# Eight scatters, the first two shared tiles, two low parts and nine loads moved around the end of an attention stage

## The reference

```python
x = x + tanh(g_xattn[0]) * L0_xattn(layernorm(x), ctx, mask)
x = x + tanh(g_ffn[0])   * L0_ffn(layernorm(x))
x = x + tanh(g_xattn[1]) * L1_xattn(layernorm(x), ctx)
x = x + tanh(g_ffn[1])   * L1_ffn(layernorm(x))
# L0_ffn, 1600 tokens, 8 experts, F = 192
scores = sigmoid(x @ W_gate_router)
sel = top_k(scores + expert_bias, 2)          # two experts for each token
w = scores[sel] / (scores[sel].sum() + EPS)
out = silu(x @ Wg_s) * (x @ Wu_s) @ Wd_s      # shared expert, every token
out += w[j] * (silu(x @ Wg[e]) * (x @ Wu[e]) @ Wd[e])   # for both chosen e
```

## Time and profile before

| what | us |
|---|---|
| median of 3 runs | 849.26 (846.79 to 850.47) |
| the profiled execution's own time | 849.73 |
| its span in the trace | 847.9 |
| PE busy | 767.5 (91%) |
| DVE busy | 578.1 (68%) |
| ACT busy | 470.4 (55%) |
| POOL busy | 214.4 (25%) |

### The profile page before, as it was taken

The page is one execution under the profiler, slowest core; times in us unless marked ns, Lnnn a source line. Parts: engine busy times, 40 slices in busy tenths (PEclk is TensorE's granted clock), DMA queues, the critical chain, the costliest instruction groups (busy, mean ns, idle before and its releaser), DMA issues.

```text
span 847.9 us, 22220 instructions
## 1 busy us (share of the span) xinstructions
PE 767.5 (91%) x7992; PEld 600.1 (71%) x7992; DVE 578.1 (68%) x1774; ACT 470.4 (55%) x1015; POOL 214.4 (25%) x212
## 2 busy tenths in 40 slices
PE   5879999999999888599998669999999898889997
PEld 2547777777767665379996457677777676669996
DVE  3877777777777676475544778787888687575433
ACT  2455666566555466345662346666666575565553
POOL 2553322133232314700005444322411210100000
PEclk9999999999999999999999869999999999999999
DMA  7899878778776903723325787887987987300001
GB/s 194 175 228 215 165 166 166 153 161 177 158 180 129 219 19 111 204 72 110 119 89 133 136 160 166 190 177 150 200 175 169 202 167 160 81 2 2 20 20 39
DMA packets 153765, 117.87 MB, mean 139 GB/s; under 512 B 81574, under 2 KB 145170, under 8 KB 153650
## 3 DMA queue, kind: packets, MB, share of 16 engines
q1 hardware_dynamic: 146410, 107.93, 58.2%
q0 software_dynamic: 4096, 6.57, 3.2%
q10 hardware_dynamic: 3152, 1.96, 1.0%
HBM read 76.17 MB, written 38.30 MB: 135 GB/s over the span
## 4 chain that ended last, share of the span: by engine, by line
PE 68%; DVE 10%; DMA 6%; issue 5%; ACT 5%; SPq 4%; ACTq 1%; another core or an unknown queue 1%; POOL 1%; DVEq 0%
PE ps L1986 21%; PE ps L2130 8%; PE ps L2104 7%; PE ps L2153 6%; PE ps L2163 6%; DMA scr_q<-qp 3%; PE ps L2149 3%; PE ps L2187 3%; DVE mx L1590 2%; DVE ps L1586 2%; ACT prob L1020 2%; SPq L478 2%; DMA QS<-scr_q 2%; PE ps L2057 2%; PE ps L2428 1%
## 5 line engine op out<-in xcount | busy, mean ns | idle before, releaser
L1020 ACT ACTIVATE prob<-ps 128x400 f32<-128x400 f32 (+1 forms) x384 | 182.4, 500 | 94.1 <-PE ps L2153 84.1
L2130 PE MATMUL ps<-KS,QS 96*100 96x361 bf16 x512 | 165.1, 338 | 17.8 <-DMA QS<-scr_q 5.5
L1586 DVE CUSTOM_DVE_ANT_0 ps<-ps,biasq 100x361 f32<-100x361 f32 x256 | 135.2, 542 | 51.7 <-PE ps L2130 43.4
L1590 DVE TENSOR_REDUCE mx<-ps 100x1 f32<-100x361 f32 x256 | 127.1, 527 | 47.0 <-PE ps L2130 40.4
L2153 PEld LDWEIGHTS ps<-QS,KS 98*128 98x128 bf16 x1536 | 108.6, 100 | 52.0 <-issue 9.7
L2153 PE MATMUL ps<-QS,KS 98*128 98x100 bf16 x1536 | 133.3, 210 | 9.0 <-ACT prob L1020 5.3
L2104 PE MATMUL ps<-cT,wk 128*128 128x361 f32 x256 | 96.6, 487 | 8.2 <-PEq L2399 6.8
L2130 PEld LDWEIGHTS ps<-KS,QS 96*100 96x100 bf16 x512 | 63.7, 126 | 53.2 <-DVE mx L1590 14.5
L730 POOL TENSOR_TENSOR kp<-kr,kp 128x722 bf16<-128x722 f32 x32 | 48.7, 1523 | 185.2 <-ACT kp L991 184.9
L2163 PE MATMUL ps<-prob,V 128*17 128x100 f32 (+1 forms) x3072 | 81.9, 256 | 0.1
L2163 PEld LDWEIGHTS ps<-prob,V 128*17 128x17 f32 (+1 forms) x3072 | 66.6, 100 | 12.7 <-issue 8.9
(11 more groups left out here) (225 smaller groups left out, 1598.1 us busy)
## 6 DMA issues: line engine op xcount, KB each, us to landing
scr_k<-kp SPq DMA_DIRECT2D x93, 180.5 KB
KS<-scr_k SPq DMA_DIRECT2D x62, 270.8 KB, 3.8
cT<-in_ctxT SPq DMA_DIRECT2D x32, 361.0 KB
KS<-scr_k SPq DMA_DIRECT2D x62, 180.5 KB, 4.2
QS<-scr_q SPq DMA_DIRECT2D x60, 150.0 KB, 4.6
KS<-scr_k SPq DMA_DIRECT2D x62, 90.2 KB, 4.4
scr_q<-qp SPq DMA_DIRECT2D x42, 100.0 KB, 5.2
xg<-scr_x SPq DMA_DIRECT2D x32, 128.0 KB
```

What stands on the lines that cost most here:

```text
L1020: nc.scalar.activation(prob[0:KROWS[t], t, hg, :], ps[0:KROWS[t], c % 2, 0:HQ * S], ACT.Exp).then_inc(a["exp"], 1)
L1586: nc.vector.tensor_tensor_reduce(ps[0:S, banks[h % len(banks)], 0:S2], ps[0:S, banks[h % len(banks)], 0:S2], biasq[p][:, :], 1.0, -3.0e38, ...
L1590: nc.vector.reduce_max(mx[:, h:h + 1], ps[0:S, banks[h % len(banks)], 0:S2], axis=AX.X).then_inc(a["max"], 1)
L2130: mm(ps[0:S, banks[h % len(banks)], 0:S2], QS[p][0:SROWS, h, :], KS[p][0:SROWS, h * S2:(h + 1) * S2], start=True, stop=True).then_inc(a["s ...
```

## The change

- **Scatters.** Steps 14 and 15 of the first attention issue four scatters each instead of two (0 to 15 are then done inside attention). POOL's wait for the end of attention goes away; scatters 16 to 25 come next, then the normalization constants of pair 7, then 26 to 31.
- **First tiles.** PE does `up(0)` and `up(1)` around the last batch's `turn_o`, ahead of `turn_on` and `project_o`; ACT loads the Silu table after `high_piece(4)` (by a Silu on one column) and does `silu(0)` before `copy_on`; DVE does `gate_up(0)` between pieces 3 and 4, ahead of the last `add_attention`.
- **Low parts.** All 12 are on DVE: 3 and 4 ahead of the last sum, 5 in loop 3, 6 in loop 5, 7 in loop 6, 8 and 9 in loop 7, 10 and 11 in loop 8. PE's wait for POOL's pieces goes.
- **Loads.** The two context loads follow `rows_store(0)` and `rows_store(2)`; the four weights and the three small loads follow `rows_store` of 4, 6, 8, 10 and 12.
- **Result rows and shares** are spread over loops 13 to 18 instead of all in loop 13.

```diff
-        SCATTERS = {8: (0,), 9: (1,), 10: (2,), 11: (3,), 12: (4, 5), 13: (6, 7), 14: (8, 9), 15: (10, 11)}
+        SCATTERS = {8: (0,), 9: (1,), 10: (2,), 11: (3,), 12: (4, 5), 13: (6, 7), 14: (8, 9, 10, 11), 15: (12, 13, 14, 15)}
...
             sp.wait_ge(sa[0]["x"], START + B)
-            ctx_load(1, 0, 0, True)
-            ctx_load(1, 1, 1, True)
             zero_fill()
-            later_weights()
...
                 rows_store(i)
+                if i in (0, 2):
+                    ctx_load(1, i // 2, i // 2, True)
+                if 4 <= i < 14 and i % 2 == 0:
+                    later_weights(i // 2 - 2)
...
                     norm_pair(F0, NPAIR - 2)
-                    pool.wait_ge(sa[0]["pv"], START + NHG * (B + 1))
...
-            for i in range(12, 15):
+            for i in range(16, 26):
                 scatter(i // 2, i % 2)
             norm_pair(F0, NPAIR - 1)
-            for i in range(15, 20):
-                scatter(i // 2, i % 2)
-            for j in POOL_PIECES:
-                low_piece(j)
-            for i in range(20, 2 * B):
+            for i in range(26, 2 * B):
                 scatter(i // 2, i % 2)
...
                     high_piece(4)
+                    nc.scalar.activation(ahead[:, :], gates[:, 0:1], ACT.Silu)
                     high_piece(5)
+                    silu(0)
...
-                    for j in range(3, NFIRST):
-                        low_piece(j)
+                    low_piece(3)
+                    gate_up(0)
+                    low_piece(4)
                 add_attention(l, B - 1)
...
                     if n == 3:
-                        low_piece(8)
+                        low_piece(5)
...
-                    if 7 <= n < 10:
-                        low_piece(n + 2)
-                    if n == NSH + 2:
-                        result_rows()
-                        shares()
+                    if 5 <= n < 7:
+                        low_piece(n + 1)
+                    if 7 <= n < 9:
+                        low_piece(2 * n - 6)
+                        low_piece(2 * n - 5)
+                    if NSH + 2 <= n < NSH + 5:
+                        result_rows((2 * (n - NSH) - 4, 2 * (n - NSH) - 3))
+                    if NSH + 5 <= n < NSH + 8:
+                        shares(((0,), (1, 2), (3, 4))[n - NSH - 5])
...
-                turn_o(l, B - 1, B - 1)
...
-                else:
-                    turn_on(l, B - 1)
-                    project_o(l, B - 1)
...
+            up(0, None)
+            turn_o(0, B - 1, B - 1)
             pe.wait_ge(s0["sc"], START + scored(NPAIR - 1))
+            up(1, None)
+            turn_on(0, B - 1)
+            project_o(0, B - 1)
             pe.wait_ge(s0["rt"], START + route_base(NPAIR - 2) + 10)
             pe.wait_ge(s0["tab"], START + 2)
             items(0, NSH)
-            pe.wait_ge(s0["plo"], START + len(POOL_PIECES))
-            pe.wait_ge(s0["wlo"], START + NPIECES - len(POOL_PIECES))
+            pe.wait_ge(s0["wlo"], START + NPIECES)
             items(NSH, NI)
```

More of the change, by code:

```diff
@@ L894, in norm, with silu @@
                 nc.scalar.activation(xT[:, :, g * GT:(g + 1) * GT], ps[:, bank:bank + KT, 0:GT], ACT.Copy).then_inc(sn["xT"], 1)
+            def silu(n):
+                rows = rows_of(n)
+                act.wait_ge(s0["up"], START + n + 1)
+                act.wait_ge(s0["h"], START + max(n - 1, 0))
+                nc.scalar.activation(sg[n % 2][0:rows, :], ps[0:rows, 2 + n % 2, 0:F], ACT.Silu).then_inc(s0["silu"], 1)
             def score_pair(j):
@@ L1187, in _ @@
             attn(0)
[L1189 to L1193, removed]
             def token_high(n):
@@ new lines, in result_rows @@
+                for k in parts:
+                    if k == 0:
+                        dve.wait_ge(s0["tab"], START + 9)
+                        nc.vector.tensor_tensor(first[:, :], upto[:, :], tiles[:, :], ALU.subtract).then_inc(r, 1)
+                        continue
+                    dve.wait_ge(r, START + base + k)
+                    if k == 1:
+                        nc.vector.scalar_tensor_tensor(first[:, :], first[:, :], float(TM), regions[:, :], ALU.mult, ALU.subtract).then_inc(r, 1)
+                    elif k == 2:
+                        nc.vector.tensor_tensor(place[:, :, :], place[:, :, :], bc(first[:, :].unsqueeze(1), [S, B, E]), ALU.add).then_inc(r, 1)
+                    elif k == 3:
+                        nc.vector.tensor_tensor(bsc[:, :, :], oh[:, 0, :, :], place[:, :, :], ALU.mult)
+                        nc.vector.tensor_tensor(mx8[:, :, :], oh[:, 1, :, :], place[:, :, :], ALU.mult).then_inc(r, 1)
+                    elif k == 4:
+                        nc.vector.reduce_sum(sj[:, 0, :], bsc[:, :, :], axis=AX.X)
+                        nc.vector.reduce_sum(sj[:, 1, :], mx8[:, :, :], axis=AX.X).then_inc(r, 1)
+                    else:
+                        nc.vector.tensor_copy(yposi[:, :, :], sj[:, :, :]).then_inc(r, 1)
@@ L1652, in low_piece, with gate_up @@
                 nc.vector.tensor_tensor(lo, raw, hi.bitcast(F32), ALU.subtract).then_inc(s0["wlo"], 1)
+            def gate_up(n):
+                rows = rows_of(n)
+                dve.wait_ge(s0["silu"], START + n + 1)
+                dve.wait_ge(s0["hT"], START + max(n - 1, 0))
+                nc.vector.tensor_tensor(hx[n % 2][0:rows, :], ps[0:rows, 2 + n % 2, F:2 * F], sg[n % 2][0:rows, :],
+                                        ALU.mult).then_inc(s0["h"], 1)
             def last_step0(b):
@@ L1844, in _ @@
             dve.wait_ge(sa[0]["x"], START + B)
-            def gate_up(n):
-                rows = rows_of(n)
-                dve.wait_ge(s0["silu"], START + n + 1)
-                dve.wait_ge(s0["hT"], START + max(n - 1, 0))
-                nc.vector.tensor_tensor(hx[n % 2][0:rows, :], ps[0:rows, 2 + n % 2, F:2 * F], sg[n % 2][0:rows, :],
-                                        ALU.mult).then_inc(s0["h"], 1)
             def token_low(n):
@@ L2374, in attn @@
                     logits(l, 2)
-                turn_o(l, B - 1, B - 1)
-                if l == 1:
+                    turn_o(l, B - 1, B - 1)
                     turn_logits(l, 1)
```

78 lines of the change are left out of this document (32 added, 46 removed).

## The result

| | us |
|---|---|
| before, median of 4 runs | 848.02 (845.16 to 850.47) |
| after, median of 4 runs | 856.38 (853.12 to 864.26) |
| ratio, 95% interval | 1.0098 (1.0055 to 1.0141) |
| profiled execution after | 853.65, span 851.8 |

A forecast was written before the change was run, and what follows sets the result against it. An unnamed stall of ACT and DVE, then PE's pace, was taken to bound the feed-forward stage. Terms +0.4 - 1.8 - 5.5 + 0.8 + 0.3 - 1.8 = -7.6 gave a median of 841.7 us, range 837.5 to 847.5.

The forecast's parts named there:

- Without the stall PE alone would turn rows six loops later: Feed-forward stage: with the unnamed stall gone, PE alone would turn rows at 357.1 and start the expert tile at 359.7.
- rival D: Last attention step: ten scatters in a row stall ACT (7.9) and DVE (5.0), 12.9 us more, 854.6; chance 0.06.
- The hole and the new load on DVE: Feed-forward loops, `up(5)` to first expert tile: 20.7 us instead of 26.2, so -5.5 (bounds -9.2 and -0.4).
- the low parts: Ahead of `up(5)`: POOL's two low parts go to DVE, so `up(5)` comes earlier, -1.8 us (bounds 0 and -2.7).
- DVE becomes the bound: Feed-forward loops 5 to 8: DVE needs 13.8 us where PE needs 9.6; PE waits 1 to 3 us in loops 8 to 10.
- Scatters in steps 14 and 15: Attention steps 14 and 15: two more scatters delay batch 15's keys, +0.3 us (bounds 0 and +2.6).
- First tiles: Around the last attention sum: two tiles brought forward buy nothing, the sum comes 0.4 us later, +0.4 (bounds -0.6 and +1.4).
- Spread: Expert tiles from loop 13: result rows and shares in six pieces remove PE's wait and slow loop, -1.8 us (bounds 0 and -1.8).
- loads behind: Feed-forward loops: two context loads moved between row loads cost +0.8 us together (bounds 0 and 1 each); the rest 0.
- The SBUF rule: Low parts beside scatters: VectorE and GpSimd shut each other out in SBUF, so four scatters would end 3.8 us later.

The follow-up runs named there:

- e15: The changed kernel, unedited, run again; no stall in its profile: 844.74 us, ratio 1.0004 to the kernel before at 845.20.
- set 1: The runs of the result itself: the kernels before and after, before at 848.0 us; stalls in both profiles.
- set 3: Runs of e5, e6, e7 and e8 on one chip, beside before at 847.59 us; stalls in all four profiles.
- e14: The changed kernel with scatters put back as before, plus ten more POOL scatters into an unused table in the last attention step: 837.88 us, ratio 0.9974.
- e2: The kernel before with only the scatters changed as in the change: 838.52 us, ratio 1.0011 to before at 837.83.
- e7: The kernel before without POOL's wait for the end of attention (scatters 12 to 25 in a row) and with result rows spread: 851.52 us, ratio 1.005.
- e8: The same kernel as e7, with the loads moved behind as well: 848.89 us, ratio 1.0009 to before at 847.59.
- e18: The changed kernel with its scatters put back as before, run a third time: 844.13 us, ratio 0.9989 to before at 845.20.
- e1: The changed kernel with the scatters alone put back as before: 838.09 us, ratio 1.001 to before at 837.83.
- e6: The changed kernel, unedited, run again in a set with stalls: 856.08 us, ratio 1.0079 to before at 847.59.
- set 6: Runs of e19 and e20, beside before at 845.05 us; e19 shows stops of PE of 2.17 and 1.69 us.
- Sets 4 and 6: Set 4 ran e11, e12, e13 and e14 beside before at 840.85 us, no stalls; set 6 has its own line.
- e12: The changed kernel with its scatters put back as before, run a second time: 840.45 us, ratio 0.9977 to before at 840.85.
- e16: Same kernel as e14 (scatters as before, ten more into an unused table), run again: 841.76 us, ratio 0.9949 to before at 845.20.
- e20: The kernel before with scatters thinned out, result rows spread and loads moved behind: 836.79 us, ratio 0.9913 to before at 845.05.
- e17: The kernel before with scatters thinned out and result rows spread, run a second time: 835.56 us, ratio 0.9877 to before at 845.20.
- e13: The changed kernel with scatters as before, plus ten plain SP writes into an unused table in the last attention step: 835.72 us, ratio 0.9957.
- e11: The kernel before with scatters thinned out and result rows spread, first run: 834.19 us, ratio 0.9924 to before at 840.85.
- e19: The kernel before, unchanged, run for a third profile: 846.03 us, ratio 1.0011 to before at 845.05.
- e5: The kernel before, unchanged, run for a second profile: 848.53 us, ratio 1.0004 to before at 847.59.

## Why the prediction was wrong, step by step

- **The step that failed** is the one that let the stall go: "Without the stall PE alone would turn rows six loops later". The hole did go, and what it was went elsewhere: the sum has no term for the ten scatters (16 to 25) beside the last attention step. Against rival D the prediction had put that the ten scatters "meet neither the zero fill nor a load"; they stalled the last steps with DMA at 0.18 while the engines stood. D's price was 12.9, ACT's and DVE's stops added; measured are 9.5 (37.9 less 28.4) and 11.8 (40.1 less 28.3), of which 1.3 is the early tiles (29.6 against 28.3 where nothing stalls). The mechanism of D was right and its price partly luck. Against e15 the profile after is 8.3 longer in the last steps. From `turn_o(13)` to `turn_o(14)` it is 3.5, and 2.4 of that are ACT's stop, 3.41 where e15 waits 1.05 for PE. From there to `turn_o(15)` it is 4.8, where PE stops twice more (0.60 and 0.95) and then works at clock 0.50. Nor did the ten stand in a row, as D has it: POOL issued four, four and two, with waits of 5.2 and 5.5 us for their rows between.
- **The hole and the new load on DVE, with the low parts: -7.3 in two terms.** To the first expert tile it is -6.2 in set 1 and -8.9 in set 3 (0.9 of each belongs to the early tiles). The size was right. From `up(5)` to the expert tile the profile after took 21.2 us, where 26.2 had been and 20.7 was forecast. That DVE becomes the bound was right too: the three waits for `hx` are there (0.70, 0.39, 1.69), and kernels in which DVE has all twelve parts take 38.1 to 39.7 (e14 alone 36.4), those with two parts on POOL and the scatters done early 35.1 to 35.3 (e2, e7, e8). So moving the low parts hardly gave 1.8 (no run moves them alone); beside scatters that are done early the kernels that have it are 3 us or more longer on this way.
- **Scatters in steps 14 and 15: +0.3, bounds 0 and +2.6.** Mis-sized, and outside its bounds: 3.4 (21.1 to 21.3 against 17.8 where nothing stalls; 1.9 in the first pair of profiles, as before stood at 19.4 in its own). The prediction followed the keys of batch 15, and they were not late. In step 14 POOL also makes pair 5's constants, behind everything else; two scatters more are 2.6, and PE stood 2.5 for them. The rest goes with the clock, 0.75 in e15's stretch from 289 to 294 where e18 has 1.00.
- **First tiles, +0.4.** Right: `turn_o(15)` is 1.3 later, `up(2)` comes 7.26 behind it in e1 where it came 8.19 behind before, so +0.3.
- **Spread, -1.8, and loads behind, +0.8.** About right. The expert tiles take 69.1 to 69.3 in the four profiles without the spread (median 69.2), 67.1 to 68.0 (67.5) in three with it and the loads ahead, and 68.1 to 70.4 (68.4) in 13 with both. That is -1.7 and +0.9, read from single executions that differ by up to 1.8 for one kernel (after 68.2, e6 70.0).
- **The sum** of the first profile: 2.7 us were lost ahead of step 14 by chance (the first `turn_o` came at 74.5 after and at 71.6 before), then +1.9, +9.4, -6.2 and -1.0, which makes 6.8 at the last expert tile. Behind it the span wins 2.9 in the last shared tiles and the second attention, which the change touches only by the loads that feed them; what won it isn't shown. The medians, which average over such chance, have 8.4.

**What stays open.** Why some sets stall and others don't. As far as one profile for each kernel can tell, it is a property of the set, not of an execution: the step from `turn_o(11)` to `turn_o(12)`, with two scatters in every kernel, takes 17.58 to 17.60 us in all six profiles of sets 1 and 3, 17.48 and 17.56 in set 6, and 17.14 to 17.16 in all twelve of the sets without stalls. The record numbers the chips of sets 2 to 6 as 4, 3, 8, 0 and 8. Sets 4 and 6 bear the same number, and only set 6 has stalls, so if that is the same chip, the chip alone doesn't decide. The changed kernel with its scatters put back (e1, e12, e18) ran in sets without stalls alone, so that its whole 1% comes back with them isn't shown either. Nor is it shown by which path a scatter holds ACT and PE: e14 and e16, built for this, ran in sets without stalls. The SBUF rule that the prediction weighed (the Trainium skill, "SBUF — State Buffer", section "SBUF: two separate sides") is about VectorE against GpSimd, and would leave ACT and PE free; the rows of e6 have ACT held for 4.22 us and PE for 3.79, so it isn't the whole of this stall. The packets of instruction fetches that the profile shows don't tell: from 300 to 340 us the profile after has none on one of the two queues that carry them, and one each in the stretches from 308, 320 and 332 (2 us long) on the other. Two of these lie beside stops, but e15 has three as well, in those from 306, 316 and 326, and doesn't stop. Whose fetches they are the profile doesn't say, so a late fetch of ACT isn't ruled out. And that thinned-out scatters escape the stalls is shown only in the weakest of the sets with stalls (e20: 30.6 in the last steps, 28.4 for e17 in a set without).

## What to carry to other kernels

A stall without a name is a property of what runs beside it until an experiment says otherwise: before moving the suspect into a tighter place, move it alone and see whether the stall follows. When work is put ahead of others on an in-order engine, list everything that this engine still does in that step, the small operations that come last above all, since each of them has a waiter. And where the kernel before takes 838 to 848 us from one set of runs to the next, a gain of 1% is only a gain if it holds in several sets: the thinned-out scatters did, together with the spread result rows (0.9924, 0.9877, 0.9913); the change lost in two sets and was level in the third (1.0098, 1.0079, 1.0004). One set is not enough for half a per cent either: e13 and e16 only add work to a kernel that is level with before, and came out 0.4 and 0.5% under it with intervals that leave out 1.

## What was not expected of the hardware

- In some sets of runs ACT, DVE and PE stop for 1 to 8 us with no named cause while POOL issues indirect DMAs; in others the profile of the same program shows no such stop (e6: 4.22 us at one instruction, e15: none at the same one).
- Such a stall needs no busy DMA engines: their share was 0.18 while ACT and PE stood in the last attention step, and 0.22 beside the same scatters where nothing stood.
- Four indirect DMAs in a row took POOL 5.1 us in either kind of set (321.06 to 326.15 in e6, 315.31 to 320.46 in e15); what differs is what the other engines do meanwhile.
